# A graph layer's MLP stage: another order of first layer, outputs and turns, and stores waited for one by one

## What is computed

```python
    def _L0_gnn_ref(x, edge_index, edge_attr, u, batch, W1, b1, W2, b2):
        ...
        summed = jax.ops.segment_sum(edge_attr, col, num_segments=x.shape[0])
        count = jax.ops.segment_sum(jnp.ones((edge_attr.shape[0],), dtype=x.dtype), col, num_segments=x.shape[0])
        agg = summed / jnp.maximum(count, 1.0)[:, None]
        h = jnp.concatenate([x, agg], axis=-1)
        h = jax.nn.relu(h @ W1 + b1)
        return x + h @ W2 + b2
    ...
    xn = _layernorm(x, axis=-1)
    x = x + _L0_gnn_ref(xn, ...) + _L0_mix_ref(xn[None], ...)[0]
    x = x + _L0_ffn_ref(_layernorm(x, axis=-1)[None], ...)[0]
```

## Time and profile before

| | us |
|---|---|
| median of 3 runs | 2540.11 (2531.42 to 2542.01) |
| profiled execution: its time / its span | 2538.14 / 2536.5 |
| PE busy in the span | 2244.4 (88%), mean granted clock 0.864 |
| DVE / ACT / POOL busy | 1366.7 / 608.8 / 1383.9 |
| MLP stage, first output to the last | 1937 to 2360 |

### The profile page before, as it was taken

One profiled execution on the slowest core, in us unless ns is written; L12 is line 12 of the kernel. 1 busy time (PEld: TensorE's weight loads), 2 busy tenths in 40 slices (PEclk: granted clock), 3 DMA queues, 4 the chain that ended last, 5 costly groups with the idle time before them and its releaser, 6 DMA issues. The chain is left out here.

```text
span 2536.5 us, 37152 instructions
## 1 busy us (share of the span) xinstructions
PE 2244.4 (88%) x10937; PEld 1620.4 (64%) x10937; DVE 1366.7 (54%) x4068; ACT 608.8 (24%) x1358; POOL 1383.9 (55%) x952
## 2 busy tenths in 40 slices
PE   2999999999999899989999489888866888898598
PEld 2888888888888633523235377777754666677386
DVE  4344444444443189854456356656656666765375
ACT  2333232323222100021111121222113333332210
POOL 1777777777778467874447777777750111111100
PEclk8999999999999899785555577778896999999799
DMA  9777777777777778697778999999955555452584
GB/s 292 144 161 160 161 166 162 158 160 159 160 153 151 196 177 206 114 287 196 185 185 177 202 185 206 206 179 226 203 93 195 176 176 156 141 171 91 185 306 168
DMA packets 535859, 455.05 MB, mean 179 GB/s; under 512 B 337456, under 2 KB 386624, under 8 KB 535763
## 3 DMA queue, kind: packets, MB, share of 16 engines
q1 hardware_dynamic: 407970, 399.37, 54.6%
q0 software_dynamic: 127792, 54.60, 21.1%
HBM read 278.77 MB, written 175.08 MB: 179 GB/s over the span
## 5 line engine op out<-in xcount | busy, mean ns | idle before, releaser
L248 POOL DMA_INDIRECT table<-edge_sums,edge_row x831 | 1308.6, 1575 | 571.1 <-issue 275.7
L195 DVE SCALAR_TENSOR_TENSOR edge_sel<-edge_dst_all,edge_dst_f,upper 128x128 f32<-128x128 int32 x831 | 328.4, 451 | 73.9 <-PE edge_sum L207 66.4
L207 PEld LDWEIGHTS edge_sum<-edge_attr,edge_sel 128*128 128x128 f32 x1662 | 254.8, 230 | 134.2 <-DVE edge_sel L195 66.4
L305 PE MATMUL pr_out_bank<-pr_norm_xT_hi,pr_w_hi 128*128 128x512 f32 (+1 forms) x832 | 326.1, 392 | 0.0
L207 PE MATMUL edge_sum<-edge_attr,edge_sel 128*128 128x65 f32 x1662 | 271.6, 317 | 54.5 <-DVE edge_sel L195 50.2
L305 PE MATMUL pr_out_bank<-pr_norm_xT_lo,pr_w_hi 128*128 128x512 f32 (+1 forms) x832 | 318.9, 383 | 0.0
L305 PE MATMUL pr_out_bank<-pr_norm_xT_hi,pr_w_lo 128*128 128x512 f32 (+1 forms) x832 | 318.5, 383 | 0.0
L217 ACT ACTIVATE edge_sums<-edge_sum 128x260 f32<-128x260 f32 (+1 forms) x209 | 80.7, 386 | 859.6 <-PE edge_sum L207 794.2
L1886 POOL DMA_DIRECT2D x_rows<-gn_x x49 | 26.9, 548 | 274.7 <-DMA x1n_T<-gn_x1nT 161.3
L305 PEld LDWEIGHTS pr_out_bank<-pr_norm_xT_lo,pr_w_hi 128*128 128x128 f32 x832 | 156.5, 188 | 31.6
L305 PEld LDWEIGHTS pr_out_bank<-pr_norm_xT_hi,pr_w_lo 128*128 128x128 f32 x832 | 157.0, 189 | 28.5
(11 more groups left out here) (193 smaller groups left out, 3920.0 us busy)
## 6 DMA issues: line engine op xcount, KB each, us to landing
edge_dst_all<-in_dst SPq DMA_DIRECT2D x103, 512.0 KB
edge_attr<-in_edge_attr SPq DMA_DIRECT2D x103, 256.0 KB
qk_T<-pr_stage SPq DMA_DIRECT2D x48, 512.0 KB
h_pre_T<-pr_stage SPq DMA_DIRECT2D x48, 512.0 KB
nm_qk<-qk_T SPq DMA_DIRECT2D x24, 1024.0 KB
sc_qk<-qk_T SPq DMA_DIRECT2D x24, 1024.0 KB
qk_scaled_T<-sc_qk SPq DMA_DIRECT2D x24, 1024.0 KB
gn_pre<-h_pre_T SPq DMA_DIRECT2D x12, 2048.0 KB, 11.4
```

What stands on the lines that cost most here:

```text
L195: op = dve.scalar_tensor_tensor(out=self.sel[q][0:rows, j, 0:rows], in0=self.dst_all[k][0:rows, t:t + m * (rows - 1) + 1:m], scalar=self.d ...
L207: mm = pe.matmul(self.p_sum[q][0:rows, j * ECOLS:(j + 1) * ECOLS], self.sel[q][0:rows, j, 0:rows], self.attr[k][0:rows, j0 + j, :], start= ...
L248: pool.indirect_dma_start(self.c.table[t], bass.IndirectOffsetOnAxis(ap=self.row[k][0:rows, j:j + 1], axis=0), self.sums[k][0:rows, j, :], ...
L305: mm = pe.matmul(out, a, c, start=first and i == 0, stop=last and i == n - 1)
```

## The change

All of it is in `gnn_stage`. On PE, three banks for the first layer instead of two (`j % BANKS`), the slots dealt out as (0, 1), (2, 3, 4), (5, 6, 7), and another order in a block: hidden 0 1, output 1, turn 0, hidden 2 3 4, output 2, turn 1, hidden 5 6 7, output 3, turn 2, turn of the aggregate of b + 2, output 0 of block b + 1, turn 3. On DVE the first half comes ahead of the `add_pre` of its subtile; `divide_sums` is cut in two, the sum of the tables at s = 0 and the division at s = 1; `split_agg` stays at the end. `add_pre` waits for `h_ready` in addition, since `hidden` no longer waits for the `hid` buffer. On ACT the third `rectify` of a subtile stands ahead of `turned`. On POOL each store is waited for right behind its issue, and the store of `x1nT(s - 1)` comes behind that of `x1(s)`.

```diff
         AHEAD = 2
+        BANKS = 3
+        SLOTS_OF = ((0, 1), (2, 3, 4), (5, 6, 7))
...
-        h_bank = [bank(f"h{k}") for k in range(2)]
+        h_bank = [bank(f"h{k}") for k in range(BANKS)]
...
                 cut = slice(j * P, (j + 1) * P)
                 if j == 0:
                     pe.wait_ge(agg_ready, b + 1)
-                pe.wait_ge(hid_ready, b * JH + j + 1)
-                pe.matmul(h_bank[j % 2][:, 0:n], w1_hi[:, cut], agg[k][:, 0:n], start=True, stop=False)
-                pe.matmul(h_bank[j % 2][:, 0:n], w1_lo[:, cut], agg[k][:, 0:n], start=False, stop=True
+                pe.wait_ge(hid_ready, b * JH + max(j, AHEAD))
+                pe.matmul(h_bank[j % BANKS][:, 0:n], w1_hi[:, cut], agg[k][:, 0:n], start=True, stop=False)
+                pe.matmul(h_bank[j % BANKS][:, 0:n], w1_lo[:, cut], agg[k][:, 0:n], start=False, stop=True
                           ).then_inc(h_mm, 1)
...
             def output(b, k, n, s):
                 r = subtiles(n)[s]
                 cut = slice(s * P, s * P + r)
-                pe.wait_ge(h_ready, b * JH + JH)
+                pe.wait_ge(h_ready, b * JH + (JH + AHEAD))
                 pe.wait_ge(x1_ready, b * CH + s + 1)
...
+            output(0, 0, BT, 0)
 
             def body(b, k, n, after):
                 ns = len(subtiles(n))
-                for s in range(CH):
+                for s in range(1, CH):
+                    if after:
+                        for j in SLOTS_OF[s - 1]:
+                            hidden(b + 1, 1 - k, after, j)
                     if s < ns:
                         output(b, k, n, s)
-                    if after:
-                        hidden(b + 1, 1 - k, after, 2 * s)
-                        hidden(b + 1, 1 - k, after, 2 * s + 1)
-                    if 1 <= s < ns:
                         turn_x1(b, n, s - 1)
-                    if s == 2 and later_size(b, 2):
-                        turn_agg(b + 2, later_size(b, 2))
+                if later_size(b, 2):
+                    turn_agg(b + 2, later_size(b, 2))
+                if after:
+                    output(b + 1, 1 - k, after, 0)
                 turn_x1(b, n, ns - 1)
 
...
             def body(b, k, n, after):
                 ns = len(subtiles(n))
                 for s in range(CH):
-                    if after:
-                        rectify(b + 1, 1 - k, after, 2 * s)
                     if s < ns:
                         deviation1(b, n, s)
-                    if after:
-                        rectify(b + 1, 1 - k, after, 2 * s + 1)
+                    if after and s < len(SLOTS_OF):
+                        for j in SLOTS_OF[s]:
+                            rectify(b + 1, 1 - k, after, j)
                     if 1 <= s < ns:
                         turned(b, n, s - 1)
-                    if s == 2 and later_size(b, 2):
-                        agg_high(b + 2, k, later_size(b, 2))
+                if later_size(b, 2):
+                    agg_high(b + 2, k, later_size(b, 2))
                 turned(b, n, ns - 1)
 
...
-            def divide_sums(b, n):
+            def add_tables(b, n):
 
                 r, ns = subtiles(n)[-1], len(subtiles(n))
                 dve.wait_ge(table_in, b * (16 * TABLES) + 16 * TABLES)
-                if not isinstance(b, int) or b >= 1:
-                    dve.wait_ge(agg_turned, b)
-                    dve.sem_inc(c.passed, 1)
                 dve.tensor_reduce(agg_sum[0:r, 0:ns, :], agg_raw[0:r, :, 0:ns, :].rearrange("p t s e -> p s e t"),
                                   AX.X, ALU.add).then_inc(agg_step, 1)
+
+            def divide_sums(b, n):
+
+                r, ns = subtiles(n)[-1], len(subtiles(n))
                 dve.wait_ge(agg_step, b * 4 + 1)
                 dve.tensor_scalar(agg_cnt[0:r, 0:ns], agg_sum[0:r, 0:ns, EDIM], 1.0, None, ALU.max).then_inc(agg_step, 1)
                 dve.wait_ge(agg_step, b * 4 + 2)
                 dve.reciprocal(agg_inv[0:r, 0:ns], agg_cnt[0:r, 0:ns]).then_inc(agg_step, 1)
                 dve.wait_ge(agg_step, b * 4 + 3)
+                if not isinstance(b, int) or b >= 1:
+                    dve.wait_ge(agg_turned, b)
+                    dve.sem_inc(c.passed, 1)
...
+                dve.wait_ge(h_ready, b * JH + j + 1)
+                dve.scalar_tensor_tensor(out=hid[j % 2][:, 0:n], in0=h_bank[j % BANKS][:, 0:n], scalar=b1[:, j:j + 1],
...
+            dve.sem_inc(h_ready, AHEAD)
...
+            add_tables(0, BT)
             divide_sums(0, BT)
...
+            add_tables(1, BT)
             divide_sums(1, BT)
             split_agg(1, 1, BT)
 
             def body(b, k, n, after):
                 ns = len(subtiles(n))
+                ahead = later_size(b, 2)
                 for s in range(CH):
-                    if after:
-                        add_pre(b + 1, 1 - k, after, 2 * s)
                     if s < ns:
                         first_half(b, k, n, s)
-                    if after:
-                        low(b + 1, 1 - k, after, 2 * s)
-                        add_pre(b + 1, 1 - k, after, 2 * s + 1)
+                    js = SLOTS_OF[s] if after and s < len(SLOTS_OF) else ()
+                    for j in js[:2]:
+                        add_pre(b + 1, 1 - k, after, j)
                     if s < ns:
                         second_half(b, n, s)
-                    if after:
-                        low(b + 1, 1 - k, after, 2 * s + 1)
+                    for i, j in enumerate(js):
+                        low(b + 1, 1 - k, after, j)
+                        if i + 2 < len(js):
+                            add_pre(b + 1, 1 - k, after, js[i + 2])
+                    if ahead and s == 0:
+                        add_tables(b + 2, ahead)
+                    if ahead and s == 1:
+                        divide_sums(b + 2, ahead)
                     if 1 <= s < ns:
                         add_part(b, s - 1)
-                    if s == 1 and later_size(b, 2):
-                        divide_sums(b + 2, later_size(b, 2))
-                    if s == 3 and later_size(b, 2):
-                        split_agg(b + 2, k, later_size(b, 2))
+                if ahead:
+                    split_agg(b + 2, k, ahead)
                 add_part(b, ns - 1)
 
...
+            def store_x1(b, n, s):
+                r = subtiles(n)[s]
+                pool.wait_ge(x1_ready, b * CH + (AHEAD + s + 1))
+                pool.sem_inc(c.passed, 1)
+                pool.dma_start(c.x1[bass.ds(b * BT + s * P, r), :], x1[s % 2][0:r, :]).then_inc(x1_stored, 16)
+                pool.wait_ge(x1_stored, b * (16 * CH) + 16 * (s + 1))
+                pool.sem_inc(x1_free, 1)
+
+            def store_x1nT(b, n, s):
+                r = subtiles(n)[s]
+                pool.wait_ge(x1nT_ready, b * CH + (AHEAD + s + 1))
+                pool.sem_inc(c.passed, 1)
+                pool.dma_start(c.x1n[:, bass.ds(b * BT + s * P, r)].rearrange("(c p) t -> p c t", p=P),
+                               x1nT[s % 2][:, :, 0:r]).then_inc(x1nT_stored, 16)
+                pool.wait_ge(x1nT_stored, b * (16 * CH) + 16 * (s + 1))
+                pool.sem_inc(x1nT_free, 1)
+
             def body(b, k, n, after):
-                for s, r in enumerate(subtiles(n)):
-                    at = b * BT + s * P
-                    pool.wait_ge(x1_ready, b * CH + (AHEAD + s + 1))
-                    pool.sem_inc(c.passed, 1)
-                    pool.dma_start(c.x1[bass.ds(at, r), :], x1[s % 2][0:r, :]).then_inc(x1_stored, 16)
-                    pool.wait_ge(x1nT_ready, b * CH + (AHEAD + s + 1))
-                    pool.sem_inc(c.passed, 1)
-                    pool.dma_start(c.x1n[:, bass.ds(at, r)].rearrange("(c p) t -> p c t", p=P), x1nT[s % 2][:, :, 0:r]
-                                   ).then_inc(x1nT_stored, 16)
-                    pool.wait_ge(x1_stored, b * (16 * CH) + 16 * (s + 1))
-                    pool.sem_inc(x1_free, 1)
-                    pool.wait_ge(x1nT_stored, b * (16 * CH) + 16 * (s + 1))
-                    pool.sem_inc(x1nT_free, 1)
+                ns = len(subtiles(n))
+                for s in range(ns):
+                    store_x1(b, n, s)
+                    if s >= 1:
+                        store_x1nT(b, n, s - 1)
+                store_x1nT(b, n, ns - 1)
 
```

More of the change, by code:

```diff
@@ L1767, in _ @@
         def _(dve):
+            def add_tables(b, n):
+                r, ns = subtiles(n)[-1], len(subtiles(n))
+                dve.wait_ge(table_in, b * (16 * TABLES) + 16 * TABLES)
+                dve.tensor_reduce(agg_sum[0:r, 0:ns, :], agg_raw[0:r, :, 0:ns, :].rearrange("p t s e -> p s e t"),
+                                  AX.X, ALU.add).then_inc(agg_step, 1)
             def divide_sums(b, n):
                 r, ns = subtiles(n)[-1], len(subtiles(n))
-                dve.wait_ge(table_in, b * (16 * TABLES) + 16 * TABLES)
-                if not isinstance(b, int) or b >= 1:
-                    dve.wait_ge(agg_turned, b)
```

(6 more changed lines are left out.)

## The result

| | before | after |
|---|---|---|
| median, 11 runs each | 2536.2 us (2528.9 to 2542.0) | 2546.3 us (2538.4 to 2548.3) |
| ratio, 95% interval | | 1.0035 [1.0021, 1.0050], some 9 us slower |
| span of the profiled execution | 2536.5 us | 2544.8 us |
| period of a block, `base` load to `base` load, mean of 9 | 35.26 us | 35.98 us |

The account below looks back on a forecast made before the run. PE, with holes, was taken to bound the kernel before, POOL's serial stores after. Intervals of 322.3 us (+5.0) and an end of 91.9 us (+7.8) gave +12.8 us on the 2540.1 us median: 2553 us, range 2515 to 2576.

Parts of the forecast that it names:

- rival 2: Gains and losses cancel: slowed stores add 4.8 us a block on POOL, period 34.6 us, 2540 us; chance 0.17.
- POOL's idle time put down to landings of both kinds: Sign on POOL: all its idle time in the stage goes to DMA landings, of x_rows too; before, 158.0 us for `x1nT` only.
- the clock under 0.94: Sign on PE: its granted clock in the stage falls below the 0.94 of before.
- the distances over 35.5 us: Sign on SP: successive loads of `base` lie over 35.5 us apart.
- the new reason for `gn_turn`'s wait: Sign on PE: `gn_turn` waits on x1n some us a block, now for another reason.
- the POOL sum: POOL's block of eight serial landings: 29.8 us quiet plus 6.4 us under loads, 36.2 us against 35.26 before.
- E: Extra time of POOL's stores beside SP's loads: 6.4 us a block, between 3.4 and 8.7.
- The first interval: Block 0's fourth `x1` to block 1's, shortened to 33.0 us because POOL starts without backlog.
- The end, the mis-sized term: Block 9's fourth `x1` to the last store's landing: 91.9 us against 84.1 before, +7.8 us.
- DVE's loop: DVE's block, closed by `add_part(3)` waiting for the last turn: 28.8 us, under POOL's quiet 29.8.
- The third bank: On PE's first layer, removes the wait of `hidden` for `add_pre` two slots back; costs nothing.
- Rival 1: POOL's serial stores are not slowed by loads: its 29.8 us sets the period, 2492 us; chance 0.22.

Follow-up runs that it names:

- e2: The kernel before with only POOL's new program, each store waited for behind its issue: 2546.0 us, ratio 1.0029 to the kernel before.
- e3: The changed kernel with POOL's stores in pairs, X(s) and N(s - 1) issued together, then both waited for: 2484.6 us, ratio 0.9775 to the kernel before.
- e7: The changed kernel, serial stores kept, with `pre` and `base` each loaded as 256 KB from block 2 on: 2498.6 us, ratio 0.9858 to the kernel before.
- e4: The changed kernel, serial stores kept, with `pre` loaded as 256 KB instead of 2 MB from block 2 on: 2518.3 us, ratio 0.9916 to the kernel before.
- e10: The changed kernel with paired stores, also across the block's end, and `add_part(3)` left in place: 2470.1 us, ratio 0.9752 to the kernel before.
- e9: The changed kernel with paired stores, also across the block's end, and `add_part(3)` behind the next block's first subtile: 2465.6 us, ratio 0.9733 to the kernel before.
- e11: A repeat of e9's kernel on the same chip as e10: 2465.3 us, ratio 0.9724 to the kernel before.
- e6: e3 with two first-layer banks instead of three, `hidden` waiting for the `add_pre` two slots back: 2531.9 us, ratio 0.9999 to the kernel before.

## Why the prediction was right, point by point

**The number.** It is less good than the mechanism. The forecast's own band began at 2546 us, and 2546.3 was measured, halfway between 2553 and the 2540 us of rival 2; the largest single chance, 0.42, stood on a loss of over 0.5%, and it is 0.35%. What tells the forecast from rival 2 is the period, 36.0 us (36.2 and 34.6).

**The direction and the mechanism.** The step on which it turned was POOL's: each store waited for behind its issue. e2 and e3 show it from both sides, the one by adding it alone (1.0029), the other by taking it away (0.9775). POOL's idle time put down to landings of both kinds (229 of the 278 us listed, not all of it as the forecast had it), the clock under 0.94, the distances over 35.5 us and the new reason for `gn_turn`'s wait were all to be seen.

**The terms of the POOL sum.** Its 36.2 us came out: from X2 to X2 POOL's block is (2291.24 - 2001.70) / 8 = 36.2 us in the mean, and (2293.17 - 2001.96) / 8 = 36.4 by the loads of `base`. But that is two errors that cancel, which was luck. Quiet, an X has a pitch of 3.1 us (3.2 forecast) and an N one of 3.9 to 4.3, mostly 4.1 (4.26 was taken from one pair of rows, at the high end): 4 x (3.1 + 4.1) = 28.8, and with a somewhat longer hand-over at the block's end 29.2 us, not 29.8. E, what the landings take over their quiet times, is 7.0 us and not 6.4; e7 and e4 split it into 1.8 us with tables and remnants alone, 2.0 more with `base` and 3.2 more with `pre`. "A store and a half fully and the third in part" was wrong in its make-up: in every block but the first of these eight just two stores pay, one X (2.7 to 3.4 us) and one N (3.0 to 4.5), and the third, 14 us or more behind `base`, lands quiet in 2.3 us. An X issued ahead of the window does escape, but then the next two pay. Two full stores, 6.7 us, had been weighed and set aside. The first interval was 32.6 us for 33.0:

```profile
1969.34 0.37 SPq L1611 DMA_DIRECT2D gn_base<-base_rows  x1
```
```profile
2293.17 0.37 SPq L1611 DMA_DIRECT2D gn_base<-base_rows  x1
...
2323.49 0.24 SPq L1614 DMA_DIRECT2D gn_base<-base_rows  x1
```

**The end, the mis-sized term.** From block 9's fourth `x1` to the last landing the forecast had 91.9 us. The last store went out at 2376.13 and took 3.1 us, so it was 2376.13 + 3.1 - (2293.17 - 0.92) = 87.0 us, 4.9 less. By POOL's own row, block 10 took 2323.18 - 2291.24 = 31.9 us where 29.8 + 4 were put, and block 11 2354.04 - 2323.18 = 30.9 where 29.8 + 2 were. Over their quiet times the landings took 3.6 and 3.4 us, so the extras were about right in sum; what was too long is the quiet sum, 28.3 and 27.5 us there. The other terms are the start, where the first store had gone 1.0 us before block 9's fourth `x1` and not 0.6 behind it (1.6 us), and 0.5 us in the last seven stores. The intervals went the other way: block 0's fourth `x1` came 0.3 us later instead of 0.35 earlier, and the nine took 323.8 us, 1.9 us over the forecast together. The expert stage behind the last landing was about 1.2 us shorter than in the profile of before, for which there was no term. With that the profiled executions are 8.3 us apart (2544.8 and 2536.5), the ratio says 8.9, and the forecast said 12.8.

**DVE's loop.** 7.1 us for subtile 0 and 7.6 for subtile 1 were 6.96 (2125.16 to 2132.12) and 7.81 in the trace of after. The loop itself was hidden there. Where POOL has slack and the loop is closed (e10), the period is 30.3 us against the 28.8 forecast for it. Where it is open too (e9, e11), PE holds with 28.9 and 29.4 us, of which it is busy 28.6 to 28.7 at full clock, against 27.5 to 28 forecast. Both terms were up to 1.5 us short, and neither was on the path of the change itself.

**The third bank.** It was put at "costs nothing", and that PE may run three hidden slots in a row was called hidden under DVE's loop. The second is wrong once POOL is out of the way: with the stores in pairs and without the bank the block is 4.2 us longer (e6 against e3), more than the stall of 3.49 us that the reordering is for the earlier trace rows. The changed kernel has the bank, so the forecast's number wasn't touched.

**The rivals.** Rival 1, stores not slowed in series, is refuted by the landings (7.1 and 5.5 us with one store in flight) and by e4 and e7. The rule of the Trainium skill that spoke for it (DMA: Bandwidth & Descriptors, "Queues, rings and completion order" and "Anatomy of one DMA"), by the prediction's estimate, puts a store of 256 KB at some 3.2 us when half the turns go to a load; the rows show 5.5 and 7.1 us, and the measurement decides. Quiet, its 2.6 us lies between the 2.3 and 3.3 us of the two layouts. The time of rival 1, 2492 us, is about where e3 lands, by another way.

## What to carry to other kernels

When a reordering lets an engine run ahead, look at the queue that nobody thinks of as busy: an engine that waits for a DMA's landing before it issues the next is occupied for the whole latency, though its busy share says 15%. Count the landings per period, quiet and beside the loads, and compare the sum with the period that you hope for. And price the parts apart. In the new order, stores in pairs instead of in series were worth 5.2 us a block and the third bank 4.2; with serial stores or without the bank the time was that of before or a little over it, and with the old store program 1% under it. What the bank or other pairs would bring in the old order was not run.

## What the hardware showed that was not expected

The slow-down of a store beside loads depends on when it is issued, to a microsecond or so. In the changed kernel's nine periods the stores of `x1` that were issued 1.1 to 1.9 us ahead of `base` landed in 2.3 us, one issued 0.3 us ahead in 3.1, and those issued from 0.1 us ahead to 1.0 us behind in 5.0 to 5.7. The N issued 1.3 us behind it took 7.1. And it isn't explained by a second store in flight, which had been a possible reading of the 6.6 us: it is there in full with one. Why a store pays 3 to 4 us here is not shown.
